# Graph attention on one core: in one of six tile groups TensorE forms the lower kind from all counts and a negated operand, its program is written without a loop, and the last block of counts is stored in the next phase

## The chip, the cores and the metric

The program runs on one core of one Trainium2 chip. The time is device microseconds of one execution; three executions of the kernel before took 2093.18, 2094.25 and 2087.33 us, so the median is 2093.18 us. A further execution was profiled, and all durations below come from it.

## The reference, cut to what matters

The reference is two rounds of graph layer and feed-forward layer over 3125 nodes with 256 features; the edge list has 103125 entries with self-loops. Only the first graph layer, a GAT attention with 4 heads of 64 columns, is touched:

```python
e = e_src[:, src] + e_dst[:, dst]
e = jnp.where(e > 0, e, NEG_SLOPE * e)            # NEG_SLOPE = 0.01
ex = jnp.exp(e_h - m[dst])                        # m: maximum per dst
den = jax.ops.segment_sum(ex, dst, num_segments=N)
out = segment_sum(ex / den[dst] * z_h[src], dst)  # z = h @ W, per head
```

The exponential of a leaky sum splits: where e_src + e_dst is above zero, it is a product of a factor of the source and one of the destination; where it is below, it is a product of two other factors. So with a matrix of edge counts (source by destination), cut into an upper kind (the counts where the sum is positive) and a lower kind (the rest), a head is two matrix products: upper kind times z scaled by the first source factor, lower kind times z scaled by the second. The destination factors come in afterwards.

## The kernel before, in words

The phases before the change: keys of the edges are cut into rows, and `count_phase` builds the matrix `counts` (3125 by 3125, bf16) by one-hot products in five blocks j of QB = 625 columns. Blocks lie in SBUF in `k.blk` (j = 0, 2, 4) and `blk_odd` (j = 1, 3). For each of the 25 tiles of 125 columns a transposed row tile goes to `countsT` in DRAM (L801), and at the end of each block the whole block goes to `counts` (L805), all issued by SyncE (SP). SP leaves the phase when the stores of `countsT` have landed (L808). The last block stays in `k.blk`, and the next phase begins with it. That is why its blocks b are numbered so that `data(b)` is block 4 first, then 0 to 3.

Between the phases stands a branch (L2408 to L2419): a rare case with more windows takes the first side, and this input takes `gat_separable_phase`. Its work is 20 sets, one for each block b and head h. A set walks the T = 25 row tiles in six groups m of 4, 4, 4, 4, 4 and 5 tiles (GROUPS), which pass through three slots (RING) of the buffer `kinds`, so that group m uses the slot that group m - 3 had. In each group

- ScalarE writes a mask per tile from the source and destination terms (L1367): zero where the sum is below zero, something large where it is above;
- VectorE takes the minimum of mask and counts, which is the upper kind (L1398), and subtracts it from the counts, which is the lower kind (L1400, releases `kinds_done`);
- TensorE multiplies, for each of the tiles and each of the 5 column tiles u, the upper kind (e = 0) and the lower kind (e = 1) with z, 195 columns wide (three bf16 parts of 65 columns), into two halves of one PSUM bank (L1480). That is 250 products in a set.

ScalarE may write group m into its slot when TensorE is through with group m - 3 (`group_done`; for m = 2 it waits for the end of the whole set before, `bank_done`). At the end of a set ScalarE scales the lower half (L1345) and VectorE adds the scaled upper half (L1408), then three parts are added (L1413, L1415). In the first set of the blocks after the first, VectorE also divides (L1419 to L1423) and adds to x (L1428), and in the second set it takes row statistics (L79 to L84). SP loads the counts of the next block into `k.blk` group by group during the last head of a block (L1314), and x at the start of the phase (L1318). TensorE, ScalarE, VectorE and SP each run a loop over the blocks; TensorE's covers all five (L1467), with one block of 1000 products as its body.

Of the kernel before, what the change touches and what calls it, by code (L numbers as in the profile page):

```python
# [5 lines left out]
BF16 = mybir.dt.bfloat16  # L6
FP32R = mybir.dt.float32r
I32 = mybir.dt.int32
ALU = mybir.AluOpType
# [3 lines left out]
N = 3125  # L13
P = 125
T = N // P
U = 5
# [552 lines left out]
def count_phase(k):  # L569
# [6 lines left out]
    with scope(nc) as (sb, pb, sem):  # L576
# [23 lines left out]
        with nc.Block() as block:  # L600
# [183 lines left out]
            @block.sync  # L784
            def _(sp):

                sp.sem_inc(blk_stored, 64)
                sp.sem_inc(tr_stored, 64)
                sp.sem_inc(z_read, 1)
                for lo_, hi_ in SPLIT:  # L790
                    sp.dma_start(k.ed_b[lo_:hi_, :, :],
                                 k.ed_dram[:, (U - 1) * U:T, :].rearrange("h t p -> h (t p)").unsqueeze(0).to_broadcast([hi_ - lo_, HEADS, QB]))\
                        .then_inc(k.ed_first, 16)
                for j in range(U):
                    with sp.Fori(0, U) as w:
                        i = j * U + w

                        sp.wait_ge(tr_done, NTB * (i + 1) + 2)
                        sp.wait_ge(tr_stored, 32 * i + 64)
                        for lo_, hi_ in SPLIT:  # L800
                            sp.dma_start(k.countsT.rearrange("(t p) s -> t p s", p=P)[bass.ds(i, 1), lo_:hi_, :].rearrange("a p s -> (a p) s"),  # L801
                                         tr[lo_:hi_, bass.ds(i % 2, 1), :].rearrange("p a s -> p (a s)")).then_inc(tr_stored, 16)
                    sp.wait_ge(blk_stored, 32 * j + 64)
                    for lo_, hi_ in SPLIT:
                        sp.dma_start(k.counts[:, j * QB:(j + 1) * QB].rearrange("(t p) d -> p t d", p=P)[lo_:hi_],  # L805
                                     blk[j % 2][lo_:hi_, :, :]).then_inc(blk_stored, 16)

                sp.wait_ge(tr_stored, 32 * T + 64)  # L808
# [60 lines left out]

def clear_low_phase(k):  # L870
# [393 lines left out]
def gat_separable_phase(k):  # L1264
# [7 lines left out]
    SHARED, OWN = (3, 4), (0, 1, 2)  # L1272
    SETS = U * HEADS
    with scope(nc) as (sb, pb, sem):
# [7 lines left out]
        mv = sb("set_bn_mv", [P, U, 2], FP32)  # L1282
        ps = pb("ps_sets", [128, 8, 512], FP32)
# [15 lines left out]
        with nc.Block() as block:  # L1299
            @block.sync  # L1300
            def _(sp):
# [14 lines left out]

                for lo_, hi_ in SPLIT:
                    sp.dma_start(k.X[lo_:hi_, :, :], k.x.rearrange("(t p) f -> p t f", p=P)[lo_:hi_]).then_inc(x_in, 16)  # L1318

                sp.wait_ge(k.blk_stored, 32 * U + 64)  # L1320
                with sp.Fori(1, U) as b:
# [4 lines left out]
                    for m in range(NM):  # L1326
# [4 lines left out]
                        sp.wait_ge(kinds_done, T * (HEADS * b - 1) + sum(GROUPS[m]))  # L1331
# [57 lines left out]
            def _(dve):  # L1389
                def make_kinds(b, h, m):  # L1390
# [7 lines left out]
                    v.tensor_tensor(out=kinds[:, lo:hi, 0, :], in0=kinds[:, lo:hi, 0, :], in1=cnt[:, t0:t0 + n, :], op=ALU.min)  # L1398
# [52 lines left out]

                block_kinds(0, True)
# [12 lines left out]
            def _(pe):  # L1465
                parts = zparts(k)
                with pe.Fori(0, U) as j:  # L1467
                    for h in range(HEADS):
                        q = HEADS * j + h
                        for m, (t0, n) in enumerate(GROUPS):  # L1470
                            pe.wait_ge(kinds_done, T * q + t0 + n)
                            turns = [OWN, SHARED] if m == 0 else [SHARED, OWN] if m == NM - 1 else [range(U)]
                            for some in turns:
                                for s in range(n):
                                    t = t0 + s
                                    for u in some:
                                        if t == 0:
                                            pe.wait_ge(bank_free, U * q + ORDER.index(u) + 1 + (U if u in SHARED else 0))
                                        for e in range(2):
                                            last = t_.matmul(ps[0:P, BANK[h % 2][u], e * W3:(e + 1) * W3],  # L1480
                                                             kinds[:, slots(m)[0] + s, e, u * P:(u + 1) * P],
                                                             parts[:, t, h, e, :, :].rearrange("p c d -> p (c d)"),
                                                             start=(t == 0 and e == 0), stop=(t == T - 1 and e == 1))
# [975 lines left out]
```

## Time and profile before

| | us |
|---|---|
| median of three executions | 2093.18 |
| profiled execution | 2089.4 |
| span of its trace | 2087.8 |
| TensorE, VectorE, ScalarE busy in the span | 1720.9, 1268.9, 1131.3 |
| the attention phase, first to last product | 470.9 to 968.6 |
| no product between the phases | 445.5 to 470.9 |

The span is cut into stages that follow each other, and each has its own limit, so the busy shares of the whole tell little about one phase. A window of the phase is read by what each engine did in it, and a timeline by what ended an engine's idle time. A name behind an arrow is the last release that the profile can see, and it may have been given long before the idle time ended; then something else, such as the reading of instructions, held the engine. "q" behind an engine's name means its sequencer, which issues and branches.

### The profile page before, as it was taken

How to read it: one execution, taken by the hardware profiler on the slowest of the kernel's cores; microseconds unless marked ns; L12 is line 12 of the kernel's file. 1: busy time of each engine (PE TensorE's matmuls, PEld its weight loads, DVE VectorE, ACT ScalarE, POOL GpSimd, SP SyncE). 2: the span in 40 equal slices, each digit the busy share in tenths (PEclk: the TensorE clock that was granted, in tenths of full speed). 3: DMA queues.
4: the chain of work that ended last, by engine and by line, in shares of the span. 5: the costliest groups of instructions: out<-in, count | busy, mean ns of one | idle time of the engine just before them, and what ended most of it. 6: DMA issues, size and time to landing. Idle time of an engine off the chain costs nothing. (4 is left out here: it accounts for less than half of the span.)

```text
span 2087.8 us, 38083 instructions
## 1 busy us (share of the span) xinstructions
PE 1720.9 (82%) x12090; PEld 1469.6 (70%) x12090; DVE 1268.9 (61%) x2128; ACT 1131.3 (54%) x2039; POOL 101.0 (5%) x124
## 2 busy tenths in 40 slices
PE   0344766739888898885999969999999999987997
PEld 0234666639888888885666659997777878776785
DVE  3767888838888889886343462222332223547997
ACT  0004777748777778874333346655655555542321
POOL 2531111100000000000000000000000000000000
PEclk9866878769999999998999989999999999998998
DMA  8231555562303030301000044444554444530102
GB/s 181 34 45 50 159 158 162 161 172 52 89 14 89 13 89 13 89 1 29 1 0 0 0 115 113 105 120 121 135 135 121 117 107 121 134 95 26 31 0 62
DMA packets 139400, 170.07 MB, mean 81 GB/s; under 512 B 27151, under 2 KB 130933, under 8 KB 139155
## 3 DMA queue, kind: packets, MB, share of 16 engines
q1 hardware_dynamic: 133472, 159.60, 30.0%
q0 software_dynamic: 5808, 8.86, 2.1%
q8 instruction: 77, 1.26, 0.3%
q14 instruction: 43, 0.35, 0.1%
HBM read 122.33 MB, written 46.04 MB: 81 GB/s over the span
## 5 line engine op out<-in xcount | busy, mean ns | idle before, releaser
L1480 PE MATMUL ps_sets<-arena,kinds 125*125 125x195 bf16 x5000 | 449.9, 251 | 73.1 <-DVE kinds L1400 57.3
L1480 PEld LDWEIGHTS ps_sets<-arena,kinds 125*125 125x125 bf16 x5000 | 440.5, 139 | 82.5 <-DVE kinds L1400 40.2
L1367 ACT ACTIVATE kinds<-ed_rows,es_mask 125x625 bf16<-125x625 f32 x500 | 366.2, 808 | 100.2 <-PE ps_sets L1480 81.2
L2104 ACT ACTIVATE onewide<-onering 125x625 fp32r (+1 forms) x375 | 256.8, 721 | 196.3 <-PE oneps L1897 193.1
L1897 PE MATMUL oneps<-oneparts_b,onewide 125*125 125x512 f32 x1250 | 294.3, 396 | 0.0
L1897 PEld LDWEIGHTS oneps<-oneparts_b,onewide 125*125 125x125 f32 x1250 | 231.2, 186 | 61.1 <-DVE onefull L1993 3.1
L1398 DVE TENSOR_TENSOR kinds<-kinds,blk 125x2500 bf16<-125x2500 bf16 x120 | 182.4, 1520 | 69.9 <-ACT kinds L1367 65.1
L752 PE MATMUL ps_hist<-X 128*125 128x125 bf16 x1250 | 124.0, 258 | 79.1 <-DVE X L659 77.5
L1400 DVE TENSOR_TENSOR kinds<-blk,kinds 125x2500 bf16<-125x2500 bf16 x120 | 182.2, 1518 | 8.9
L752 PEld LDWEIGHTS ps_hist<-X 128*125 128x125 bf16 x1250 | 105.5, 168 | 95.1 <-DVE X L659 54.6
L1894 PE MATMUL oneps<-oneparts_a,onewide 125*125 125x258 f32 x625 | 152.5, 286 | 18.8 <-ACT onewide L2101 18.8
L1895 PE MATMUL oneps<-oneparts_a,onewide 125*125 125x256 f32 x625 | 151.2, 283 | 0.0
L1897 PE MATMUL oneps<-oneparts_a,onewide 125*125 125x512 f32 x625 | 148.8, 397 | 0.0
L1897 PEld LDWEIGHTS oneps<-oneparts_a,onewide 125*125 125x125 f32 x625 | 115.2, 185 | 30.2 <-DVE onetmp L1988 1.4
L1894 PEld LDWEIGHTS oneps<-oneparts_a,onewide 125*125 125x125 f32 x625 | 117.5, 188 | 19.3 <-issue 19.2
L2101 ACT ACTIVATE onewide<-onering 125x625 fp32r (+1 forms) x125 | 89.7, 720 | 61.8 <-PE oneps L1895 59.5
L1991 DVE SCALAR_TENSOR_TENSOR oneraw<-oneps,oneinv,onebias 125x256 f32<-125x256 f32 x50 | 23.9, 477 | 154.5 <-PE oneps L1897 154.5
L1895 PEld LDWEIGHTS oneps<-oneparts_a,onewide 125*125 125x125 f32 x625 | 117.7, 188 | 0.1
L659 DVE TENSOR_TENSOR X<-iota_rep,rowG 128x1250 bf16<-128x1250 bf16 x125 | 100.9, 807 | 16.0 <-issue 15.6
L659 DVE TENSOR_TENSOR X<-iota_rep,colG 128x1250 bf16<-128x1250 bf16 x125 | 100.3, 803 | 0.0
L2011 DVE COPY onefull<-oneps_w 125x512 f32<-125x512 f32 (+1 forms) x30 | 18.1, 603 | 131.8 <-PE oneps_w L1922 131.8
L704 ACT ACTIVATE tr<-ps_tr 125x500 f32 (+3 forms) x175 | 90.7, 560 | 1.0 <-PE ps_tr L762 1.0
(277 smaller groups left out, 2222.3 us busy)
## 6 DMA issues: line engine op xcount, KB each, us to landing
onering<-counts SPq DMA_DIRECT2D x50, 683.6 KB
onering<-countsT SPq DMA_DIRECT2D x50, 683.6 KB
countsT<-tr SPq DMA_DIRECT2D x25, 683.6 KB
blk<-counts SPq DMA_DIRECT2D x20, 546.9 KB
counts<-blk SPq DMA_DIRECT2D x3, 3418.0 KB
counts<-blk_odd SPq DMA_DIRECT2D x2, 3418.0 KB
ed_rows<-ed_dram SPq DMA_DIRECT2D x16, 273.4 KB
onering<-counts SPq DMA_DIRECT2D x50, 79.3 KB
```

The costliest lines, as they stand in the source:

```text
L659: v.tensor_tensor(out=hot[:, u, :, :, :], in0=iota_rep[:, :, :, :], in1=cut[:, bass.ds(i * U + u, 1), :, :].rearrange("q a g c -> q (a g) ...
L704: a.activation(tr[:, bass.ds(i % 2, 1), r * TQ * P:(r * TQ + n) * P].rearrange("p a c -> p (a c)"), ps_tr[0:P, r % 2, 0:n * P], ACT.Copy). ...
L752: last = t_.matmul(ps[0:P, PAIR[u], b, s * P:(s + 1) * P], col_hot[:, u, gg, :, c], row_hot[:, u, gg, :, c], start=(c == 0), stop=(c == 1))
L1367: a.activation(kinds[:, slots(m)[0] + s, 0, :], ed_b[:, h, :], ACT.Relu, scale=MASK_SCALE, bias=k.es_mask[:, t0 + s, h:h + 1]).then_inc(ma ...
L1398: v.tensor_tensor(out=kinds[:, lo:hi, 0, :], in0=kinds[:, lo:hi, 0, :], in1=cnt[:, t0:t0 + n, :], op=ALU.min)
L1400: v.tensor_tensor(out=kinds[:, lo:hi, 1, :], in0=cnt[:, t0:t0 + n, :], in1=kinds[:, lo:hi, 0, :], op=ALU.subtract).then_inc(kinds_done, n)
L1480: last = t_.matmul(ps[0:P, BANK[h % 2][u], e * W3:(e + 1) * W3], kinds[:, slots(m)[0] + s, e, u * P:(u + 1) * P], parts[:, t, h, e, :, :]. ...
L1894: t_.matmul(ps[0:P, kk, 0:FD], tile, rows[:, t % T, F:X2], start=(t == 0), stop=False)
L1895: last = t_.matmul(ps[0:P, kk, 0:F], tile, rows[:, t % T, 0:F], start=False, stop=(t == TB - 1))
L1897: last = t_.matmul(ps[0:P, kk, :], tile, rows[:, t % T, 0:2 * F], start=(t == 0), stop=(t == TB - 1))
L2101: a.activation(wide[:, t % RF, :], tile, ACT.Copy, accum_out=row_sums[:, bass.ds(i, 1), s, w:w + 1].rearrange("p a c -> p (a c)")).then_in ...
L2104: a.activation(wide[:, t % RF, :], tile, ACT.Copy).then_inc(wide_done, 1)
```

## The change

There are three edits in `gat_separable_phase` and one that touches `count_phase` as well.

1. For group m = 2 (WHOLE, tiles 8 to 11) VectorE makes the upper kind alone. TensorE takes three products in place of two for each tile and column tile: upper kind times the first z, upper kind times the negated second z (`minus`, written once at the start of the phase by VectorE), and all counts times the second z. The last two sum to what the lower kind gave.
2. Since TensorE now reads `cnt` itself, SP loads that group of the next block when TensorE is through with it, and after group 3 (LOADS).
3. TensorE's program is written out for all five blocks, with waits on constants.
4. The store of the last block of counts moves out of `count_phase`. In the attention phase SP issues it after the masks of the first set, and loads x after the masks of the second set; before, x was loaded at once.

```diff
--- count_phase, SP
-                    sp.wait_ge(blk_stored, 32 * j + 64)
-                    for lo_, hi_ in SPLIT:
-                        sp.dma_start(k.counts[:, j * QB:(j + 1) * QB]...).then_inc(blk_stored, 16)
+                    if j < U - 1:
+                        (the same)
 
                 sp.wait_ge(tr_stored, 32 * T + 64)
...
+def store_last_block(k, sp):
+    for lo_, hi_ in SPLIT:
+        sp.dma_start(k.counts[:, (U - 1) * QB:N].rearrange("(t p) d -> p t d", p=P)[lo_:hi_],
+                     k.blk[lo_:hi_, :, :]).then_inc(k.blk_stored, 16)
...
--- gat_separable_phase
+    WHOLE = 2
+    LOADS = (0, 1, 3, WHOLE, 4, 5)
+        minus = sb("z_minus", [P, WN, HEADS, W3], BF16)
...
+                sp.wait_ge(mask_done, T)
+                sp.wait_ge(k.blk_stored, 32 * U + 32)
+                store_last_block(k, sp)
+                sp.wait_ge(mask_done, 2 * T)
                 for lo_, hi_ in SPLIT:
                     sp.dma_start(k.X[lo_:hi_, :, :], ...).then_inc(x_in, 16)
...
+                        if m == WHOLE:
+                            sp.wait_ge(group_done, (NM - 1) * HEADS * b + m + 1)
+                        else:
+                            sp.wait_ge(kinds_done, T * (HEADS * b - 1) + sum(GROUPS[m]))
                         load_cnt(b - 1, m)
...
-                    v.tensor_tensor(out=kinds[:, lo:hi, 0, :], in0=kinds[:, lo:hi, 0, :], in1=cnt[:, t0:t0 + n, :], op=ALU.min)
+                    above = v.tensor_tensor(out=kinds[:, lo:hi, 0, :], ...same..., op=ALU.min)
+                    if m == WHOLE:
+                        above.then_inc(kinds_done, n)
+                        return
                     v.drain()
...
+                v.tensor_scalar(minus[:, :, :, :], zparts(k)[:, W0:W0 + WN, :, 1, :, :]..., -1.0, None, ALU.mult)
+                v.drain()
                 block_kinds(0, True)
...
-                with pe.Fori(0, U) as j:
+                for j in range(U):
...
-                                        for e in range(2):
-                                            last = t_.matmul(ps[..., e * W3:(e + 1) * W3], kinds[..., e, ...], parts[:, t, h, e, :, :], ...)
+                                        t_.matmul(out[0], kind[0], z[0], start=(t == 0), stop=False)
+                                        if m == WHOLE:
+                                            t_.matmul(out[1], kind[0], minus[:, s, h, :], start=False, stop=False)
+                                            last = t_.matmul(out[1], cnt[:, t, u * P:(u + 1) * P], z[1], start=False, stop=False)
+                                        else:
+                                            last = t_.matmul(out[1], kind[1], z[1], start=False, stop=(t == T - 1))
```

Where the change moves instructions is shown at three places. The first is SP from the last block of counts to the first loads of the attention phase. Before, with L805 the store of counts, L600 and L69 the ends of blocks of code, and L1318 the load of x:

```order
L801 DMA countsT<-tr 13x3125
L795 REGISTER_ALU
L795 COMPARE_AND_BRANCH
L805 DMA counts<-blk 112x25x625
L805 DMA counts<-blk 13x25x625
L600 UNCONDITIONAL_BRANCH
...
L1300 UNCONDITIONAL_BRANCH
L1318 DMA X<-in_x_dram 112x25x256
L1318 DMA X<-in_x_dram 13x25x256
```

And of the change, where L874 is the store and L1336 the load of x:

```order
L801 DMA countsT<-tr 13x3125
L795 REGISTER_ALU
L795 COMPARE_AND_BRANCH
L600 UNCONDITIONAL_BRANCH
...
L1314 UNCONDITIONAL_BRANCH
L874 DMA counts<-blk 112x25x625
L874 DMA counts<-blk 13x25x625
L1336 DMA X<-in_x_dram 112x25x256
L1336 DMA X<-in_x_dram 13x25x256
```

The two issues of the store have left the stretch between the last `countsT` and the end of the phase, and stand behind the phase's start.

The second place is VectorE in the groups m = 1, 2 and 3 of a set. Before, each group has a pair, and the additions of the set before (L1408, L1413, L1415) stand between the pairs:

```order
L1398 TENSOR_TENSOR kinds<-kinds,blk 125x4x625
L1400 TENSOR_TENSOR kinds<-blk,kinds 125x4x625
L1408 SCALAR_TENSOR_TENSOR set_both<-ps_sets,dst_exp,set_slope 125x195 x3
L1398 TENSOR_TENSOR kinds<-kinds,blk 125x4x625
L1400 TENSOR_TENSOR kinds<-blk,kinds 125x4x625
L1413 TENSOR_TENSOR set_num<-set_both 125x325
L1415 TENSOR_TENSOR set_num<-set_num,set_both 125x325
L1398 TENSOR_TENSOR kinds<-kinds,blk 125x4x625
L1400 TENSOR_TENSOR kinds<-blk,kinds 125x4x625
```

Of the change (L1419 is the minimum, L1424 the subtraction):

```order
L1419 TENSOR_TENSOR kinds<-kinds,blk 125x4x625
L1424 TENSOR_TENSOR kinds<-blk,kinds 125x4x625
L1432 SCALAR_TENSOR_TENSOR set_both<-ps_sets,dst_exp,set_slope 125x195 x3
L1419 TENSOR_TENSOR kinds<-kinds,blk 125x4x625
L1437 TENSOR_TENSOR set_num<-set_both 125x325
L1439 TENSOR_TENSOR set_num<-set_num,set_both 125x325
L1419 TENSOR_TENSOR kinds<-kinds,blk 125x4x625
L1424 TENSOR_TENSOR kinds<-blk,kinds 125x4x625
```

One subtraction is gone, in group 2; the rest keeps its order.

The third place is TensorE at the head of its loop, before (L1467 is the loop, L1478 and L1471 the waits):

```order
L1467 UNCONDITIONAL_BRANCH
L1467 ISA
L1478 ISA
L1480 MATMUL ps_sets<-arena,kinds 125x195 x2
L1478 REGISTER_ALU
```

And at the border from group 1 to group 2, of the change:

```order
L1508 MATMUL ps_sets<-arena,kinds 125x195
L1514 MATMUL ps_sets<-arena,kinds 125x195
L1508 MATMUL ps_sets<-arena,kinds 125x195
L1511 MATMUL ps_sets<-z_minus,kinds 125x195
L1512 MATMUL ps_sets<-arena,blk 125x195
L1508 MATMUL ps_sets<-arena,kinds 125x195
```

The branch is gone, and pairs become triples in group 2 alone.

## Rows read from the trace of the kernel before

**Rows 1.** The page: busy time, share of the span, instructions

```profile
PE 1720.9 (82%) x12090; PEld 1469.6 (70%) x12090; DVE 1268.9 (61%) x2128; ACT 1131.3 (54%) x2039; POOL 101.0 (5%) x124
```

**Rows 2.** The page, costliest groups: count, busy us, mean ns, idle before and its releaser

```profile
L1480 PE MATMUL ps_sets<-arena,kinds 125*125 125x195 bf16 x5000 | 449.9, 251 | 73.1 <-DVE kinds L1400 57.3
...
L1400 DVE TENSOR_TENSOR kinds<-blk,kinds 125x2500 bf16<-125x2500 bf16 x120 | 182.2, 1518 | 8.9
```

**Rows 3.** Windows (length, busy and count per engine, PEclk, DMA share, GB/s), blocks one, two, five

```profile
470.90:566.90 96.00, 88.76 (x1001) 87.23 (x1001) 85.17 (x77) 82.51 (x124) 0.00 (x0) 0.98 0.31 74
566.90:668.90 102.00, 90.56 (x1000) 88.62 (x1000) 87.97 (x91) 80.20 (x120) 0.00 (x0) 0.97 0.20 52
...
870.50:968.60 98.10, 90.65 (x1000) 88.71 (x1000) 82.39 (x86) 71.27 (x108) 0.00 (x0) 0.97 0.01 2
```

**Rows 4.** Timeline across the phase border: start, length, engine, line, count, idle before

```profile
431.70 15.29 SPq L801 DMA_DIRECT2D countsT<-tr  x6
...
447.20 7.55 SPq L805 DMA_DIRECT2D counts<-blk  x2
463.42 7.09 SPq L1318 DMA_DIRECT2D X<-in_x_dram  x2
464.79 8.59 ACT L1367 ACTIVATE kinds<-ed_rows,es_mask 125x625 bf16<-125x625 f32 x12 [19.00 <-issue]
...
470.90 18.93 PE L1480 MATMUL ps_sets<-arena,kinds 125*125 125x195 bf16 x200 [25.43 <-DVE kinds L1400]
```

**Rows 5.** Windows, a store of countsT alone, then the idle stretch at the border

```profile
434.00:435.00 1.00, 0.80 (x13) 0.80 (x14) 0.82 (x3) 1.00 (x4) 0.00 (x0) 1.00 0.83 300
435.00:436.00 1.00, 0.62 (x8) 0.49 (x5) 1.00 (x2) 1.00 (x4) 0.00 (x0) 1.00 0.03 13
...
454.80:461.50 6.70, 0.00 (x0) 0.00 (x0) 0.00 (x0) 0.00 (x0) 0.00 (x0) 0.50 1.03 291
```

**Rows 6.** Line L2419, the branch into the phase: min/median/max ns, first and last start

```profile
L2419 PEldq COMPARE_BRANCH  x1: 8168/8168/8168, 456.4 to 456.4; - x1
```

**Rows 7.** Line L2430, a later branch, and the timeline behind it

```profile
L2430 PEldq COMPARE_BRANCH  x1: 3752/3752/3752, 1216.7 to 1216.7; - x1
...
1219.99 1.28 ACT L2069 ACT_TABLE_LOAD   x1 [25.48 <-issue]
```

**Rows 8.** Line L1467, TensorE's loop

```profile
L1467 PEldq COMPARE_BRANCH  x5: 79/4865/5852, 560.7 to 966.9; - x5
```

**Rows 9.** Timeline at the end of the first block

```profile
566.88 15.34 PE L1480 MATMUL ps_sets<-arena,kinds 125*125 125x195 bf16 x160 [4.56 <-DVE set_both L1408]
...
572.13 2.94 ACT L1367 ACTIVATE kinds<-ed_rows,es_mask 125x625 bf16<-125x625 f32 x4 [5.81 <-PE ps_sets L1480]
...
583.20 1.49 DVE L1428 TENSOR_TENSOR X<-X,set_num 125x1280 f32 x1
```

**Rows 10.** Windows: after two long gaps of TensorE

```profile
566.80:570.20 3.40, 3.32 (x21) 3.33 (x22) 3.16 (x4) 0.00 (x0) 0.00 (x0) 0.52 0.02 5
...
611.00:614.40 3.40, 3.40 (x24) 3.40 (x23) 3.33 (x3) 0.27 (x1) 0.00 (x0) 0.50 0.00 0
```

**Rows 11.** Timeline, the third set

```profile
505.51 3.65 ACT L1367 ACTIVATE kinds<-ed_rows,es_mask 125x625 bf16<-125x625 f32 x5 [0.61 <-PE ps_sets L1480]
...
506.00 21.77 PE L1480 MATMUL ps_sets<-arena,kinds 125*125 125x195 bf16 x250 [0.62 <-DVE kinds L1400]
...
509.19 1.79 DVE L1398 TENSOR_TENSOR kinds<-kinds,blk 125x3125 bf16<-125x3125 bf16 x1 [0.32 <-ACT kinds L1367]
...
511.06 1.79 DVE L1400 TENSOR_TENSOR kinds<-blk,kinds 125x3125 bf16<-125x3125 bf16 x1
...
528.37 21.96 PE L1480 MATMUL ps_sets<-arena,kinds 125*125 125x195 bf16 x250 [0.60 <-DVE kinds L1400]
```

**Rows 12.** DMA queues, 440 to 1000 us: packets, MB, share

```profile
q8 instruction: 50, 0.82, 0.6%
```

**Rows 13.** Timeline, statistics of one block, behind the last set

```profile
974.75 1.73 DVE L79 BATCH_NORM_STATS2 set_bn_st<-X 125x6 f32<-125x256 f32 x5
```

More of the change, by code:

```diff
@@ L802, in _ @@
                                          tr[lo_:hi_, bass.ds(i % 2, 1), :].rearrange("p a s -> p (a s)")).then_inc(tr_stored, 16)
-                    sp.wait_ge(blk_stored, 32 * j + 64)
-                    for lo_, hi_ in SPLIT:
-                        sp.dma_start(k.counts[:, j * QB:(j + 1) * QB].rearrange("(t p) d -> p t d", p=P)[lo_:hi_],
-                                     blk[j % 2][lo_:hi_, :, :]).then_inc(blk_stored, 16)
+                    if j < U - 1:
+                        sp.wait_ge(blk_stored, 32 * j + 64)
+                        for lo_, hi_ in SPLIT:
+                            sp.dma_start(k.counts[:, j * QB:(j + 1) * QB].rearrange("(t p) d -> p t d", p=P)[lo_:hi_],
+                                         blk[j % 2][lo_:hi_, :, :]).then_inc(blk_stored, 16)
                 sp.wait_ge(tr_stored, 32 * T + 64)
@@ L867, in _ @@
                 t_.drain().then_inc(cut_psum, 1)
+def store_last_block(k, sp):
+    for lo_, hi_ in SPLIT:
+        sp.dma_start(k.counts[:, (U - 1) * QB:N].rearrange("(t p) d -> p t d", p=P)[lo_:hi_],
+                     k.blk[lo_:hi_, :, :]).then_inc(k.blk_stored, 16)
 def clear_low_phase(k):
@@ L1325, in _ @@
                         load_ed(b - 1, h)
-                    for m in range(NM):
+                    for m in LOADS:
                         if m == NM - 2:
@@ L1397, in make_kinds @@
                     dve.wait_ge(mask_done, T * q + t0 + n)
-                    v.tensor_tensor(out=kinds[:, lo:hi, 0, :], in0=kinds[:, lo:hi, 0, :], in1=cnt[:, t0:t0 + n, :], op=ALU.min)
+                    above = v.tensor_tensor(out=kinds[:, lo:hi, 0, :], in0=kinds[:, lo:hi, 0, :], in1=cnt[:, t0:t0 + n, :], op=ALU.min)
+                    if m == WHOLE:
+                        above.then_inc(kinds_done, n)
+                        return
                     v.drain()
@@ L1478, in _ @@
                                             pe.wait_ge(bank_free, U * q + ORDER.index(u) + 1 + (U if u in SHARED else 0))
-                                        for e in range(2):
[L1480 to L1483, printed above, removed]
+                                        z = [parts[:, t, h, e, :, :].rearrange("p c d -> p (c d)") for e in range(2)]
+                                        out = [ps[0:P, BANK[h % 2][u], e * W3:(e + 1) * W3] for e in range(2)]
+                                        kind = [kinds[:, slots(m)[0] + s, e, u * P:(u + 1) * P] for e in range(2)]
+                                        t_.matmul(out[0], kind[0], z[0], start=(t == 0), stop=False)
[4 more added lines that the diff above has]
+                                            last = t_.matmul(out[1], kind[1], z[1], start=False, stop=(t == T - 1))
                                         if t == T - 1:
```

5 lines of the change are left out of this document (4 added, 1 removed).

## The prediction

> **What bounds the kernel now.** I read the page first for the shares, then the costliest groups, then windows over the attention phase, then the timelines at its start, at the end of a block and inside one set.
>
> TensorE is busy 82% of the span [rows 1], but that is an average; the change touches one phase of 498 us. There TensorE's products are busy 449.9 us and VectorE's subtractions alone 182.2 [rows 2]. The five blocks take 96.0, 102.0, 101.6 (row not shown), 100.0 (likewise) and 98.1 us [rows 3]: the last four together are 968.6 - 566.9 = 401.7 us. In the second block TensorE is busy 90.6, VectorE 88.0 and ScalarE 80.2 of 102 us. So it is a ring of three engines, with TensorE ahead by little, and I ask at each place which wait ends last.
>
> A plain set is the third: its 250 products run from 506.00 for 21.77 us and the next set's start at 528.37 [rows 11], so a set takes 22.37 us, and one product (21.77 - 0.25) / 249 = 86.4 ns. The pause of 0.6 us is ended by a subtraction. Four such pauses don't explain 102 us a block. The rest lies in the first two sets of a block, where VectorE has the divisions and the statistics, and at the block's end: TensorE stands 4.56 us before 566.88 and ScalarE then 5.81 us before 572.13 [rows 9]. The release named there, VectorE's addition, was not what came last, since TensorE's own loop branch took 5.85 us at 560.7; the five are 79 (the exit), 4865 and at most 5852 ns [rows 8]. A branch back is read anew from memory. After that gap the granted clock stood at 0.52 for 3.4 us, with 21 products started where 39 fit, and the same at 611 us, behind a pause that VectorE made, at 0.50 with 24 [rows 10]. TensorE had been idle before both falls.
>
> At the phase's start nothing is computed for 19 us. SP issues the last store of countsT up to 446.99, then that of the block from 447.20 for 7.55 us [rows 4]. Until 461.5 the DMA engines are full (share 1.03 [rows 5]). TensorE's branch into the phase is given at 456.4 and takes 8.17 us [rows 6]; ScalarE's first mask stands at 464.79, the first product at 470.90 [rows 4]. A later branch of the same sort, with no store about, takes 3.75 us on TensorE, from 1216.7, and ScalarE works at 1219.99 [rows 7]. So 4.4 us of the branch are its reading of code behind 3.8 MB of counts.
>
> **The start of the phase.** Without L805, SP waits for countsT alone. A tile's store issued at 431.70 [rows 4] keeps the DMA engines at 0.83 up to 435 and at 0.03 behind it [rows 5], so it lands about 3.6 us after its issue. The last pair of issues begins near 446.2 (0.8 us before its end) and lands by about 450.2. From the end of SP's issue, 447.20 + 7.55 = 454.75, to the branch at 456.4 were 1.65 us of barriers; now 450.2 + 1.65 = 451.9. From the branch to the first mask were 3.4 us at the quiet branch (1216.6 to 1219.99): 455.3. Against 464.79 that is 9.5 us earlier. Bounds: nothing of the branch's 4.4 is saved, and 4.5 are left; or 11, if landing and barriers are shorter still. I take 9.5.
>
> The store now runs beside the first sets: SP issues 7.55 us and the DMA engines are full for some 15. Queued behind it on SP are the load of x and the ed rows; x is wanted at the end of block one, 96 us in, and the store is issued after 25 masks, so there are 40 us to spare: nothing. The negated z, 3120 elements, is new on VectorE before its first minimum. The nearest row is the 4-tile subtraction, two operands of 2500 elements in 1.46 us (below), so 3120 take 1.8 us at most. VectorE has to wait for the first four masks, 4 x 0.72 = 2.9 us at 12 masks in 8.59 [rows 4], and they cover it; without the cover it costs 1.8 us.
>
> **The loop.** Four branches back go, with gaps of 4.56 us at the first and less at the next ones (4865 ns is the median of the branches, against 5852): some 16 us of TensorE's idleness. What is late next is VectorE: a boundary set has two multiplications and additions of 1.49 us more than a plain one, as at 583.20 [rows 9], with the small steps beside them some 3.9 us. So not all of it comes back. The clock falls behind the gap should go with it; each costs 18 products of 86 ns, 1.5 us [rows 10].
>
> **The whole group.** In a set, 4 tiles of 5 column tiles get a third product: 20 of 86.4 ns, 1.73 us, so 400 in all. VectorE is rid of one 4-tile subtraction, 1.46 us (1518 ns is the mean over 120, of which 20 are of 5 tiles at 1.79 [rows 2, 11]), and of the drain before it: some 1.55 us. That would be an even exchange if both were on one path. TensorE's set now takes at least 270 x 86.4 = 23.33 us, above the 22.37 of before. And a pause stays. Group 5 uses the slot of group 2: ScalarE starts its five masks at 505.51, 0.4 us after TensorE's last product of group 2 is begun, takes 3.65, VectorE follows with two of 1.79 from 509.19 and ends at 12.85 past 500 [rows 11], that is 7.8 us after that product's start at 505.1 (the products of group 2 ended where the pause before 506.00 begins). TensorE spans it with groups 3 and 4, 80 x 86.4 ns = 6.9 us. So about 0.85 us of pause in every set, at group 5, where before it was at group 3. A plain set: 24.2 us, 1.8 more. In the first set of a block the division and the addition to x (3.9 us of VectorE) fall before group 5's pair and push it back by another 0.8: 25.0. The second set's statistics, 1.73 us [rows 13] and some 2.5 with aggregation and drains, fall before group 4 and fit into the time saved: 24.2.
>
> [...]
>
> **The sum**, on the profile's own time of 2089.4 us (span 2087.8). Block one: 96.0 less its 4.56 us of branch plus 4 x 1.8 = 98.6. The other four: 25.0 + 3 x 24.2 = 97.6 each, 390.4 in all. Together 489.0, where 497.7 were: 8.7 us less. To that some of the clock falls at 611 and its like in later blocks, which are in the 401.7 already. With the start: 8.7 + 9.5 = 18.2 us. So 2071.2 on the profile's time. The median of the runs, 2093.18, is 3.8 above the profile and the lowest, 2087.33, is 2.1 below; 2093.2 - 18.2 = 2075.0. I give 2072, between the two.
>
> **The rivals.**
> 1. The ring pauses less. If ScalarE and VectorE catch up and the pause at group 5 vanishes, a plain set takes 23.4 and 20 sets give 16 us more: 2056. For it: VectorE has 1.55 us less to do. Against it: the way from group 2 to group 5 has no subtraction of group 2 in it.
> 2. The phase's start gains only SP's issue. If the branch takes 8 us without the store too, since four engines read code at once, 4.4 to 5 us of the 9.5 are lost: 2077. Against it is the quiet branch [rows 7], where all engines branch as well.
> 3. The third product costs more than a pace. If it waits 1 us a set more, by sums into the same half bank twice in a row or by a longer way round the ring, it takes back 20 us: 2092, no change. Against it: 250 products into alternating halves of few banks keep one pace [rows 11], though none there repeats its half.
> 4. The written-out program starves TensorE, and the kernel is slower. Its code in this phase was one body read five times, 50 pages of 0.82 MB in all [rows 12]; now there are some 54 pages, none met twice. If each page held TensorE as long as the quiet branch did, 3.75 us [rows 7], it would add 200 us; it decides from about 0.4 us a page, which is 22 us. At 1 us a page: 2072 + 54 = 2126. Against it: the body of 1000 products is far more than one page too, and between the branches the third set has no gap, at 250 products in one row [rows 11]. Nor did the load of x, issued over 7.09 us beside the first 200 products, leave one in their row [rows 4].
>
> [...]
>
> **How the numbers follow.** Forecast 0.62, around 2072, own range 2065 to 2080. Rival 1: 0.12. Rival 2: 0.10. Rival 3: 0.10. Rival 4: 0.06. The range of 8 in 10 takes the forecast, rival 2 and the near half of rival 1: 2060 to 2083. Within 0.3%, 6.3 us, which is about what a measurement can tell from no change, lies rival 3 and little else: 0.09. Slower is rival 4, with a small part of rival 3: 0.05. Faster: 0.86.
>
> **What would show it.** In the new profile the first mask stands at 455 us and the first product at 461; no branch of 5 us in TensorE's program; 5400 products at 86 ns; plain sets 24.2 us apart with one pause of under 1 us, before group 5; the granted clock without falls between the first and the last set; the phase 489 us from first to last product. I am wrong if the first mask comes later than 459, if plain sets take 23.5 or 25.5, or if TensorE pauses at a place in no relation to a group's start, which would be its code.

## The result, and the profile after

Four executions of the changed kernel took 2068.73 to 2073.39 us, median 2072.01; four of the kernel before took 2087.33 to 2094.25, median 2093.64. The ratio is 0.990, with a 95% interval of 0.9881 to 0.9918. The forecast was 2072. The profiled execution took 2072.66 us, its span 2071.0.

The page of the changed kernel, busy times and costliest groups (columns as in [rows 1] and [rows 2]; L1508 is the first product of every pair or triple, L1514 the second product of the pairs, L1424 the subtraction):

```profile
PE 1745.5 (84%) x12490; PEld 1497.4 (72%) x12490; DVE 1242.3 (60%) x2109; ACT 1129.1 (55%) x2039; POOL 99.8 (5%) x124
...
L1508 PE MATMUL ps_sets<-arena,kinds 125*125 125x195 bf16 x2500 | 462.9, 247 | 33.1 <-DVE kinds L1424 33.0
L1388 ACT ACTIVATE kinds<-ed_rows,es_mask 125x625 bf16<-125x625 f32 x500 | 364.2, 808 | 69.6 <-PE ps_sets L1512 42.4
...
L1514 PE MATMUL ps_sets<-arena,kinds 125*125 125x195 bf16 x2100 | 364.4, 249 | 0.0
...
L1424 DVE TENSOR_TENSOR kinds<-blk,kinds 125x2500 bf16<-125x2500 bf16 (+1 forms) x100 | 152.9, 1529 | 7.4
```

TensorE is a little busier, VectorE has 20 subtractions less, and the waiting in front of products fell from 73.1 us [rows 2] to 33.1. The wait before the very first product is in both, 25.4 us before [rows 4] and 16.5 after, so inside the phase 47.7 us of waiting became 16.6. The windows over blocks one, two and five, as in [rows 3]:

```profile
463.00:561.00 98.00, 95.21 (x1081) 94.43 (x1082) 75.21 (x67) 78.18 (x117) 0.00 (x0) 0.97 0.53 125
561.00:657.40 96.40, 92.95 (x1082) 91.93 (x1081) 82.88 (x87) 79.91 (x121) 0.00 (x0) 1.00 0.21 55
...
850.40:947.10 96.70, 93.20 (x1082) 91.98 (x1080) 80.13 (x85) 74.47 (x114) 0.00 (x0) 1.00 0.02 4
```

The third and fourth block are as the second. The last product of the kernel before ends at 968.45, and not at 968.6, so to the end of the last product the phase lasts 484.0 us where it was 497.5; the phases of the runs below are taken in this way. Block one is 2 us longer than before, the others 5.6, 5.1, 3.5 and 1.4 us shorter. TensorE is now busy 93 of 96.4 us in a block, and from the second block on the granted clock stands at 1.00. In block one it is 0.97: the 0.50 of the idle time before the phase lasts until 5.0 us behind the first product, with 28 products started from 463.0 to 467.5 where the pace of the full clock gives 53; before, it lasted 3.6 us. A plain set is one that is neither the first of all nor the first or second of a block. Inside it one pause is left, before group 5, as this row of the timeline shows:

```profile
556.65 0.30 PE L1508 MATMUL ps_sets<-arena,kinds 125*125 125x195 bf16 x1 [0.70 <-DVE kinds L1424]
```

The start of the phase, a timeline as in [rows 4], and the branch as in [rows 6]:

```profile
447.17 0.86 SPq L801 DMA_DIRECT2D countsT<-tr  x2
456.85 0.98 DVE L1476 TENSOR_SCALAR z_minus<-arena 125x3120 bf16<-125x3120 bf16 x1 [13.71 <-issue]
456.99 3.64 ACT L1388 ACTIVATE kinds<-ed_rows,es_mask 125x625 bf16<-125x625 f32 x5 [10.16 <-SPq L1316]
459.96 1.47 DVE L1419 TENSOR_TENSOR kinds<-kinds,blk 125x2500 bf16<-125x2500 bf16 x1 [2.13 <-ACT kinds L1388]
```

```profile
L2450 PEldq COMPARE_BRANCH  x1: 3413/3413/3413, 452.9 to 452.9; - x1
```

The last store of countsT is issued at 447.17, the branch given at 452.9, and it takes 3.4 us instead of 8.2. Beside the 8.2 us stands a late packet on q8, one of the queues that the profile labels "instruction". These are rows in views of the DMA queues. Before, q8 has no packet from 456.4, the branch, to 461.4, while the store (q1) fills the engines with a share of 102.9%, and one from 461.4 to 463.4; after the change it has one from 452.9 to 455.0:

```profile
q1 hardware_dynamic: 1145, 1.42, 102.9%
...
q8 instruction: 1, 0.02, 5.1%
```

```profile
q8 instruction: 1, 0.02, 3.2%
```

The packet starts 5.2 us behind the branch before, and 1.0 us after, and TensorE's branch ends 3.0 and 2.4 us behind that start; in all 14 traces it is 2.3 to 3.3 us. That the branch waits for this packet is my reading of these times. So the 8.8 us have two parts of about the same size: SP no longer issues for 7.6 us before it leaves the phase, so the branch comes 6.4 us behind the last transposition instead of 10.9, and the branch is 4.8 us shorter; 0.4 us are lost again between its end and the first mask. The negated z takes 0.98 us and lies in front of the first minimum, which waits for masks. In this execution the phase before ended 1.0 us later, at 446.51 instead of 445.47; from there to the first mask it was 19.3 us and is 10.5. The store and the load of x come later on SP, and the store fills the DMA engines without a mark on TensorE: from 489 to 495 it starts 73 products at a DMA share of 1.01, and from 497 to 503 74 at 0.03 (the row below is the share in 40 slices of 480 to 500 us):

```profile
481.27 6.25 SPq L874 DMA_DIRECT2D counts<-blk  x2
505.14 5.70 SPq L1336 DMA_DIRECT2D X<-in_x_dram  x2
```

```profile
DMA  0000599999999999999999999998976543200000
```

So far 8.9 us from the last transposition to the first product and 13.5 in the phase, which is more than the 16.8 by which the spans differ. The rest went into the expert phase behind. From the last product of attention to the first step of the convolutions there were 252.0 us, and now there are 256.1. Windows of 8 us at the same distances behind the last product (the third 1.2 us further in the changed kernel), first before, then after:

```profile
1038.90:1046.90 8.00, 5.67 (x27) 4.07 (x27) 5.78 (x25) 2.09 (x5) 0.00 (x0) 1.00 0.00 0
1082.10:1090.10 8.00, 8.00 (x28) 6.34 (x28) 5.64 (x22) 1.15 (x3) 0.00 (x0) 0.58 0.00 0
1126.50:1134.50 8.00, 8.00 (x28) 6.47 (x28) 5.65 (x23) 1.15 (x3) 0.00 (x0) 0.58 0.00 0
1172.10:1180.10 8.00, 8.00 (x36) 5.85 (x36) 5.90 (x31) 3.24 (x7) 0.00 (x0) 1.00 0.00 0
```

```profile
1017.50:1025.50 8.00, 8.00 (x29) 6.59 (x29) 5.76 (x22) 1.05 (x3) 0.00 (x0) 0.57 0.00 1
1060.70:1068.70 8.00, 7.58 (x41) 5.65 (x39) 6.27 (x21) 1.05 (x2) 0.00 (x0) 1.00 0.00 0
1106.30:1114.30 8.00, 8.00 (x24) 6.02 (x24) 5.78 (x24) 1.43 (x4) 0.00 (x0) 0.57 0.00 0
1150.70:1158.70 8.00, 8.00 (x26) 6.14 (x26) 3.95 (x19) 1.25 (x4) 0.00 (x0) 0.58 0.00 0
```

The third number from the end of a row is the granted clock. In the first window a fall is new (0.57 against 1.00), in the second it has gone (1.00 against 0.58), in the third both have one, and in the fourth one is new. Laid over each other product by product, the two expert phases drift apart only where one has the clock at half and the other not: 1.0 us at the start, where the clock comes back later, 0.7 more by 82 us, 1.2 back at 114 us, and 3.3 at 204 us. Between these places the distance between the two stays within 0.1 us.

### The profile page after: what moved, and what is told of

Read it like the earlier page. It is cut to its first block and busy times, and to the rows that moved or that the text cites. A ratio compares the mean times of both kernels' runs of the same rounds, so it can differ in the third digit from the quotient of the medians.

```text
span 2071.0 us, 38655 instructions
## 1 busy us (share of the span) xinstructions
PE 1745.5 (84%) x12490; PEld 1497.4 (72%) x12490; DVE 1242.3 (60%) x2109; ACT 1129.1 (55%) x2039; POOL 99.8 (5%) x124
## 5 line engine op out<-in xcount | busy, mean ns | idle before, releaser
L1508 PE MATMUL ps_sets<-arena,kinds 125*125 125x195 bf16 x2500 | 462.9, 247 | 33.1 <-DVE kinds L1424 33.0
L1508 PEld LDWEIGHTS ps_sets<-arena,kinds 125*125 125x125 bf16 x2500 | 343.8, 138 | 38.1 <-DVE kinds L1424 37.9
L1514 PE MATMUL ps_sets<-arena,kinds 125*125 125x195 bf16 x2100 | 364.4, 249 | 0.0
L2135 ACT ACTIVATE onewide<-onering 125x625 fp32r (+1 forms) x375 | 256.9, 721 | 196.4 <-PE oneps L1928 193.2
L1514 PEld LDWEIGHTS ps_sets<-arena,kinds 125*125 125x125 bf16 x2100 | 282.8, 135 | 0.0
L1419 DVE TENSOR_TENSOR kinds<-kinds,blk 125x2500 bf16<-125x2500 bf16 x120 | 182.4, 1520 | 65.4 <-ACT kinds L1388 61.0
L752 PE MATMUL ps_hist<-X 128*125 128x125 bf16 x1250 | 126.8, 262 | 75.3 <-DVE X L659 73.1
L1424 DVE TENSOR_TENSOR kinds<-blk,kinds 125x2500 bf16<-125x2500 bf16 (+1 forms) x100 | 152.9, 1529 | 7.4
L1925 PEld LDWEIGHTS oneps<-oneparts_a,onewide 125*125 125x125 f32 x625 | 117.8, 188 | 19.4 <-issue 19.3
L2022 DVE SCALAR_TENSOR_TENSOR oneraw<-oneps,oneinv,onebias 125x256 f32<-125x256 f32 x50 | 23.9, 477 | 154.6 <-PE oneps L1928 154.4
```

The lines of the kernel that those rows point to most:

```text
L752: last = t_.matmul(ps[0:P, PAIR[u], b, s * P:(s + 1) * P], col_hot[:, u, gg, :, c], row_hot[:, u, gg, :, c], start=(c == 0), stop=(c == 1))
L1419: above = v.tensor_tensor(out=kinds[:, lo:hi, 0, :], in0=kinds[:, lo:hi, 0, :], in1=cnt[:, t0:t0 + n, :], op=ALU.min)
L1424: v.tensor_tensor(out=kinds[:, lo:hi, 1, :], in0=cnt[:, t0:t0 + n, :], in1=kinds[:, lo:hi, 0, :], op=ALU.subtract).then_inc(kinds_done, n)
L1508: t_.matmul(out[0], kind[0], z[0], start=(t == 0), stop=False)
L1514: last = t_.matmul(out[1], kind[1], z[1], start=False, stop=(t == T - 1))
L1925: t_.matmul(ps[0:P, kk, 0:FD], tile, rows[:, t % T, F:X2], start=(t == 0), stop=False)
```

## The experiments

Times are medians. The kernel before ran beside them on the same chip and took 2092.0 beside e1 to e4 and 2092.9 beside e5 to e8; e6 and e9 to e12 were executed once each: 2084.64, 2052.16, 2090.59, 2071.03 and 2077.26 us, where the kernel before alone spreads from 2086 to 2097. They are read by their traces, and not by these times. "The phase" is the time from its first product to the end of its last. "A set" is the time from its first product to the next set's.

### The parts one by one

**e1_no_loop**: the kernel before, with

```diff
-                with pe.Fori(0, U) as j:
+                for j in range(U):
```

> The kernel before with TensorE's program of the attention phase written out, nothing else. Theory A (the loop's branches cost what their gaps show): the phase, 497.7 us from first to last product, loses the four gaps of 16 us and some clock falls, so 478 to 485, and the kernel is 13 to 19 us faster. Rival B (VectorE is late next, so the gaps are covered and TensorE waits there anyway): 492 to 497, the kernel under 5 us faster. Rival C (the written-out program starves): pauses at places that are no group's start, and a time above before.

Measured: 2077.66 us, ratio 0.9923 (0.9899 to 0.9948). The phase took 481.0 us, 16.6 less than before. Sets at a block's end went from 27.3, 26.8, 26.3 and 26.3 to 22.5, 22.8, 22.6 and 22.6. The sets behind them changed little (26.0 and 26.1 to 26.3). The gaps were 4.6, 3.8, 3.6 and 3.5 us, 15.4 in all, and of the clock's seven falls in the phase two are left. So Theory A holds, and the whole of the gaps came back: VectorE's extra work lies in the next set, and it had not used the gap to get ahead. No pause stood anywhere but at a group's start, so rival C falls. The time gained 14.3 us and not 16.6; in the trace the expert phase (below) is 2.1 us longer. The early store is still in this kernel, and its start shows the long idle time:

```profile
448.78 7.62 SPq L805 DMA_DIRECT2D counts<-blk  x2
...
466.52 8.59 ACT L1367 ACTIVATE kinds<-ed_rows,es_mask 125x625 bf16<-125x625 f32 x12 [19.24 <-issue]
```

**e2_whole_only**: the changed kernel with

```diff
-                for j in range(U):
+                with pe.Fori(0, U) as j:
...
-                sp.wait_ge(mask_done, T)
-                ... store_last_block ...      # back at the end of count_phase
-                sp.wait_ge(mask_done, 2 * T)
```

> The kernel before with only group 2 formed by three products and its later load; the loop and the early store stay. Theory A (the third product costs a plain set 1.4 us, gives the first set of a block 1.2 and the second 2): block one 98, the other four 97 plus a branch gap of 4 to 4.5 and a clock fall, so 505 to 508 for the phase against 497.7, the kernel 6 to 10 us slower. Rival B (VectorE's saved subtraction is what shortened the phase): 484 to 492, faster by 6 to 13 us.

Measured: 2103.11 us, ratio 1.0055 (1.0034 to 1.0075), so slower. The phase took 499.3 us, 1.8 more than before, and not the 7 to 10 that I had expected from the sets. The sets were near the expected (plain 23.9, first 24.6 to 26.1, second 23.9), but the branch gaps made the last sets of the blocks only 3.0 to 4.0 us longer each, and of the falls that I had counted for each block the trace has two. The median of the times is 11 us above before's, and the trace, taken from the quickest of its executions (2093.79), shows 4.4 of them. The other executions have no trace; their mean granted clock on record is lower, 0.917 to 0.923 against 0.924, but what lengthened them is open. So these 11 us are not the price of the whole group: in the written-out program, e4_no_whole below, it is 2.8 us by the medians and 3.6 by the phase. Rival B falls in either case.

**e3_store_only**: the kernel before with only the two moves on SP,

```diff
-  (count_phase, last block)  sp.dma_start(k.counts[...], blk...)
+  (attention)                sp.wait_ge(mask_done, T); store_last_block(k, sp)
+                             sp.wait_ge(mask_done, 2 * T)
                              (load of x)
```

> The kernel before with only the store of the last block and the load of x moved later. Theory A: the first mask comes 9.5 us earlier (455.3 where 464.8 was), the phase stays at 497 to 498, the kernel 9 us faster. Rival B (the store is only moved beside the products, and slows them or their code's reading there): the phase grows by 3 us or more, and the kernel gains under 6.

Measured: 2084.75 us, ratio 0.9964 (0.9951 to 0.9977). The first mask stands at 456.0:

```profile
446.64 0.86 SPq L801 DMA_DIRECT2D countsT<-tr  x2
456.04 8.60 ACT L1386 ACTIVATE kinds<-ed_rows,es_mask 125x625 bf16<-125x625 f32 x12 [9.74 <-SPq L1314]
```

From the end of the last transposition, 446.0, that is 10.1 us instead of 19.3, so 9.2 us gained, and the phase took 497.7 us, as before within 0.2. Theory A holds for the start and for the phase. The time gained 7.2 us where it said 9; the trace has the expert phase 2.1 us longer here too.

**e4_no_whole**: the changed kernel with pairs in all groups,

```diff
-    WHOLE = 2
-    LOADS = (0, 1, 3, WHOLE, 4, 5)
+    WHOLE = -1
+    LOADS = tuple(range(NM))
```

and no `minus`.

> The changed kernel with two products in all groups: written-out program and later store, group 2 with its subtraction. Theory A (third product and subtraction about cancel): plain sets 22.5, first sets of a block 26, second sets 25.2 to 26.5, the phase 478 to 484 against 484.0 in the changed kernel, so the time is 2066 to 2072. Rival B (the whole group brings 5 us or more of the gain): the phase 489 or more, 2077 or more.

Measured: 2069.19 us, ratio 0.9879 (0.9854 to 0.9904). The windows of blocks one to three:

```profile
461.50:553.60 92.10, 89.41 (x1000) 88.05 (x1001) 80.79 (x71) 78.44 (x117) 0.00 (x0) 0.97 0.55 133
553.60:650.60 97.00, 87.86 (x1004) 85.58 (x1002) 88.60 (x91) 80.48 (x121) 0.00 (x0) 1.00 0.21 56
650.60:747.20 96.60, 87.87 (x1003) 85.60 (x1002) 88.60 (x91) 80.53 (x122) 0.00 (x0) 1.00 0.21 55
```

The phase took 480.4 us, 3.6 less than in the changed kernel. Block one, 92.1 us, is 5.8 shorter; the others, 97.0, 96.6, 98.0 and 96.7, are up to 1.5 longer. So the third products cost a little more than they bring, and the whole of the gain is from the other two parts. Theory A holds in this. The time's advantage over the changed kernel, 2.8 us, lies inside the ranges of the two.

### What the whole group does in a set

**e6_keep_sub**: the changed kernel, where VectorE subtracts in group 2 too,

```diff
-                    if m == WHOLE:
-                        above.then_inc(kinds_done, n)
-                        return
```

> The changed kernel, but VectorE makes group 2's subtraction all the same (its result is not used), so only TensorE's extra work is in it. Theory A (a plain set is set by TensorE's 270 products and the way from group 2 to group 5, which holds no subtraction of group 2; VectorE's relief counts only in the first two sets of a block): plain sets 23.9 to 24.1, first and second sets of a block 26 and 25 in place of 24.8 and 23.9, the phase 492 to 496. Rival B (VectorE's relief counts in each set): plain sets 25.4, the phase above 510.

**e9_relief_only**: pairs, where VectorE leaves out group 2's subtraction,

```diff
+                    if m == 2:
+                        above.then_inc(kinds_done, n)
+                        return
...
-   t_.matmul(out[1], kind[1], z[1], ...)
+   t_.matmul(out[1], kind[0 if m == 2 else 1], z[1], ...)
```

> Pairs in all groups, but VectorE makes no subtraction in group 2, so the lower kind of that group is left out of the result (the second product reads the upper kind again). It shows VectorE's relief without TensorE's third product. Theory A (in a plain set TensorE's 250 products and the ring set the pace, VectorE's relief counts where it has other work too): plain sets 21.9 to 22.3 where pairs alone take 22.5, first and second sets of a block 24.7 and 23.5 where they take 26.3 and 25 to 26.5, the phase 465 to 470 against 480. Rival B (VectorE bounds every set): plain sets 21.2 or less, the phase below 455.

In e9_relief_only the lower kind of group 2 is missing from the result, so it serves for timing alone. With e4_no_whole and the changed kernel they make a table of two by two, in us for a set, from the same phase of each trace:

| | plain set | first of a block | second | the phase |
|---|---|---|---|---|
| pairs, subtraction (e4_no_whole) | 22.4 to 22.8 | 26.3 | 25.1 to 26.5 | 480.4 |
| pairs, none (e9_relief_only) | 22.2 to 22.3 | 24.8 | 23.6 to 25.1 | 465.4 |
| triples, subtraction (e6_keep_sub) | 24.0 to 24.5 | 26.3 | 25.1 to 25.3 | 498.9 |
| triples, none (the change) | 23.9 | 24.8 | 23.9 | 484.0 |

In a plain set the third product costs 1.6 us and the saved subtraction brings 0.1 to 0.6, mostly 0.3. In the first set of a block it is the other way: the subtraction brings 1.5 and the third product costs nothing. In the second, 1.2 or more against 0.3 at most. Theory A of both holds, with the phase of e6_keep_sub 3 us above its range and that of e9_relief_only inside. Beside the very first set there are eleven plain ones, and four of each other kind.

### Where the pause comes from, and a better place

**e5_whole3**: the changed kernel with

```diff
-    WHOLE = 2
-    LOADS = (0, 1, 3, WHOLE, 4, 5)
+    WHOLE = 3
+    LOADS = (0, 1, 2, 4, WHOLE, 5)
```

> The changed kernel with group 3 in place of group 2 as the whole one, and its later load behind that of group 4. Theory A (the pause of 0.9 us before group 5 comes from the ring: group 5 needs the slot of the long group 2, 7.8 us of masks, minimum and subtraction against 6.9 us of products): with group 3 long, 8.5 us of products stand between group 2's end and group 5, so that pause goes; plain sets 23.0 to 23.5 where they are 23.9, the phase 472 to 477 where it is 483.8, the time 2061 to 2066. Rival B (the pause comes from the amount of work, wherever the third product stands): 23.9 and 484.

Measured: 2063.93 us, ratio 0.9861 (0.9846 to 0.9876). Plain sets 23.1 to 23.5, the phase 476.0 us. The pause before group 5 is gone in plain sets, and a shorter one before group 2, of up to 0.6 us, is there. So the pause is the ring's: it hangs on how many products stand between the end of group 2 and the start of group 5, 100 here and 80 in the changed kernel.

**e8_whole3_two_sets**: group 3, but only in the first two sets of blocks two to five,

```diff
-                    if m == WHOLE:
+                    if m == WHOLE and h < 2 and not isinstance(b, int):
...
-                                        if m == WHOLE:
+                                        if m == WHOLE and h < 2 and j > 0:
```

with WHOLE = 3 and the loads in the usual order.

> The changed kernel with the third product only where VectorE is late: in the first two sets of blocks two to five, for group 3; pairs elsewhere, and the usual order of loads. Theory A: plain sets 22.5 as with pairs alone, first sets 24.3, second 23.4, so 24.8 + 3 x 22.4 + 4 x 93.0 = 464 for the phase, some 20 us less than the changed kernel: 2050 to 2056. Rival B (the relief in two sets is eaten by the sets behind them): 475 or more, 2064 or more.

Measured: 2056.21 us over five executions (2053.89 to 2056.87), ratio 0.9819 (0.9806 to 0.9833). Windows of blocks one to three:

```profile
462.90:555.30 92.40, 89.70 (x1001) 88.34 (x1002) 80.81 (x71) 78.51 (x117) 0.00 (x0) 0.97 0.54 132
555.30:649.30 94.00, 90.29 (x1043) 88.79 (x1042) 85.65 (x89) 80.43 (x121) 0.00 (x0) 1.00 0.22 58
649.30:742.90 93.60, 90.29 (x1043) 88.79 (x1042) 85.67 (x89) 80.47 (x121) 0.00 (x0) 1.00 0.22 58
```

The phase took 467.3 us. Plain sets 22.4 to 22.8, first 24.8, second 23.6 to 23.8. First sets are 0.5 and second 0.2 longer than I had expected, which is 3 us. This version is 37 us below the kernel before, and 16 below the changed one (2072.01, timed apart from it). Of the versions whose result is complete it is the fastest.

### Does the store hurt near the start?

**e7_store_at_start**: the changed kernel without `sp.wait_ge(mask_done, T)` and `sp.wait_ge(mask_done, 2 * T)`, so store and load are issued at once.

> The changed kernel with the last store of counts and the load of x issued at the very start of the attention phase, without waits for masks. Theory A (what cost 9 us was the store standing before the branch, so that all engines' code waited behind it): the first mask stays at 456 to 457, the first set grows by 0 to 2 us, the time is within 3 us of the changed kernel. Rival B (the store hurts wherever it stands near the start, because the next pages of code are read behind it): the first set or the first mask is 4 us or more later.

Measured: 2073.64 us, ratio 0.9904 (0.9888 to 0.9920):

```profile
449.04 0.86 SPq L801 DMA_DIRECT2D countsT<-tr  x2
458.39 7.14 SPq L874 DMA_DIRECT2D counts<-blk  x2
...
458.87 3.64 ACT L1386 ACTIVATE kinds<-ed_rows,es_mask 125x625 bf16<-125x625 f32 x5 [10.17 <-SPq L1316]
```

From the end of the transpositions, 448.4, to the first mask it took 10.5 us, as in the changed kernel, and the phase 483.5. Theory A holds: what counts is that the store stands behind the branch. The waits for the masks bring nothing. The branch was given at 454.8 and took 3.3 us, so even here the first issue, at 458.39, came 0.3 us behind its end; a store issued while the branch runs was not tried.

### The expert phase

**e10_before_again** and **e11_after_again** are the two kernels once more.

> The kernel before, a second look. It tells whether the expert phase, 252 us in its first trace against 256 in the changed kernel's, is slower by the change. Theory A (the number of clock falls of 6.8 us in that phase varies from run to run, two in the first trace, three or four in the others): 254 to 258 us here too if there are three or four falls, 252 if two, so about 1.7 us for each. Rival B (the change makes that phase slower): 252 here whatever the falls.

> The changed kernel, a second look, for the same question. Theory A: its expert phase follows the number of its clock falls as in the kernel before. Rival B: 256 us again at any number. Both: the attention phase 483 to 485 from first to last product, the sets as in the first trace within 0.1 us.

Before: two falls and 252.4 us, as the first time. Changed: four falls and 256.9 us, attention 484.5. So the kernel before showed the same number twice, where I had thought it free from run to run, and the changed kernel more of them both times, though not the same number. Two executions of each are few. Over all traces the stretch goes with their number: 252.0 and 252.4 with two; 253.1 to 256.1 with three (e1, e2, e3, e5, e6, e9 and the change); 256.9 to 258.9 with four (e4, e7, e8 and the change again), counting falls of 3.4 and of 6.8 us between the long ones at the phase's start and end.

**e12_shift**: the changed kernel with one more operation of VectorE at the end of the attention phase,

```diff
+                v.tensor_tensor(out=num[:, :, :, :], in0=num[:, :, :, :], in1=num[:, :, :, :], op=ALU.max)
+                v.drain()
```

> The changed kernel with one more operation of 1.5 us on VectorE at the very end of the attention phase, on a tile that is no longer used. The expert phase behind it took 252.0 and 252.4 us with two clock falls of 6.8 us in both looks at the kernel before, 256.1 and 257.0 with three and four in both looks at the changed one, from the last product of attention to the first step of the convolutions. Theory A (which of the expert phase's pauses lead to a fall hangs on the moment at which the phase begins): the number of falls changes, and the stretch less the added 1.5 us follows it, 252 to 255. Rival B (something in the changed kernel slows the expert phase itself): 256 to 257 plus 1.5, with three or four falls again.

Three falls again and 258.7 us, 257.1 without the addition, which is above what the other traces with three falls have. The fall at 71 us was gone and that at 114 us back, as in the kernel before, but that at 204 us stayed, and the phase's start lost 1.8 us against the kernel before, where the changed kernel lost 1.0. So the number of falls alone does not give the stretch; where they stand, and how late the clock comes back at the start, count too. About the number that rival B gives came out, and Theory A's did not. Since the drift between the traces arises only at places where the clocks differ, the stretch is longer by its clock and not by its work. Why the clock falls more often there is open.

## Why the prediction was right, point by point

**The start.** Forecast 9.5 us earlier; 8.8 in the changed kernel and 9.2 in e3_store_only, counted from the end of the phase before. The branch at 3.4 us, as the quiet one's 3.75 [rows 7], and its place at 4.9 us behind SP's last issue were right. The first mask came 4.1 us behind the branch, and not 3.4.

**The loop.** Right in mechanism. The text let some of the gaps be covered by VectorE's extra work, "so not all of it comes back", while the sum's blocks of 97.6 us have nothing left of the gaps; the sum was the better of the two. e1_no_loop gave 16.6 us for gaps of 15.4 and five clock falls. The extra work stands in the set behind the border and takes its time either way.

**The whole group.** Right: in a plain set the first product of group 5 starts 0.95 us behind the last of group 4, 0.86 more than the pace, where 0.85 was forecast, and the sum gave 24.2 us where 23.9 came. The mis-sized term is the pace of a product, 86.4 ns, taken over one set. In plain sets groups 2 and 3 had 86.3 to 87.2 ns before and 84.1 to 84.5 and 85.1 to 85.8 after, the others 85 to 87 in both; a whole set less its pause now comes to 85.3. At the twelve plain or second sets of blocks two to five that is 3.7 us, and with four first sets of 24.8 for 25.0 and block one at 97.9 for 98.6 it brings the sum's 489.0 to the measured 484.0 within 0.2.

**The sum.** It held 18.2 us: 9.5 and 8.7. The traces have 8.9 and 13.5, less 1.0 that the count phase was longer by, 4.1 in the expert phase and 0.5 behind it, 16.8. I had no term for the phases behind, and what they lost hid that the phase gained 4.8 us more than the sum gave it. So the forecast of 2072 is nearer than its parts, and that is luck. By the medians the gain was 21.6. The profile before, 2089.4, lay 4 us below the median, and the forecast stood between the sum on the one, 2071.2, and on the other, 2075.0.

**The rivals.** 1 fell: the pause at group 5 is there. 2 fell: the branch took 3.4 us. 3 fell: the three products of a tile keep a pace of 84.3 ns, repeated half or not. 4 fell: q8 has 45 packets from 440 to 1000 us, fewer than before's 50 [rows 12], and none shows as a wait of a product, since at the full clock none inside a group starts more than 0.14 us behind the one before it:

```profile
q8 instruction: 45, 0.74, 0.6%
```

What the forecast did not ask is whether the third product was worth having. It was priced at 1.73 us for TensorE against 1.55 for VectorE, and the table of two by two shows that such prices say nothing alone: 0.3 us of VectorE's count in a plain set and all of TensorE's, and the reverse in a first set. Who waits for whom in the changed kernel says the same; ScalarE now waits for the last product of the whole group (L1512):

```profile
ACT kinds L1388 <- PE ps_sets L1512: 42.4, 20, 2.1
...
PE ps_sets L1508 <- DVE kinds L1424: 33.0, 24, 16.5
```

## What to carry to other kernels

Where two engines take turns at being late, move work from one to the other only in the stretches where the one is late; here the trade made in all 20 sets cost 3.6 us of the phase against pairs, and made in 8 sets, at the better group, it brought 13. In a ring of slots, put the longer group where the way to its slot's next user has products to spare: here the phase took 476.0 us with group 3 long and 484.0 with group 2. Look at what stands in the DMA queues before a branch into a new phase: here a store of 3.8 MB cost 8.8 us there, half by the time that SP took to issue it and half in a branch of 8.2 us in place of 3.4, and the same store just behind the branch cost nothing, with 10.5 us to the first mask and 483.5 for the phase against 10.5 and 484.0.

## What the runs showed of the hardware that I had not expected

The branch back over a body of 1000 products took TensorE 4.8 to 5.9 us each time in the first trace, although the target had been run before [rows 8], and left it 3.5 to 4.6 us without a product. Three new packets on q8 stand within 11 us of each of the four branches, as at 563.5, 567.3 and 571.5 behind the first at 560.7, where otherwise one comes each 6 to 14 us. In the written-out program the 45 packets on q8, one of them at 493 beside a store that filled the DMA engines for 12 us, left no gap inside a group. The first q8 packet behind the branch into the phase started 1.0 us after it with free DMA engines, and 5.2 us after it behind a store (3.4 to 5.2 in the four traces with the store before the branch, 0.9 to 1.0 in all others). The granted clock's falls in the expert phase were two in both executions of the kernel before, at the same distances behind attention within 0.1 us, and three and four in those of the changed one, where the added falls cost up to 3.3 us each.
